# FFN second layer: the bias as a matmul of 33 rows, and the sum takes tn itself

## The reference, cut to what matters

```
tn  = _ln_t(t)                               # layer norm without gain
# each sample picks 2 of 8 experts, with weights top_w
h   = gelu(tn @ W1[e] + b1[e])               # 256 -> 512, for both experts
y   = h @ W2[e] + b2[e]                      # 512 -> 256
out = sum over the two experts of top_w * y
t   = t + _layer_norm(out + tn, gamma, beta)
```

## Time and profile before

| | us |
|---|---|
| median of 3 runs (1199.36 to 1202.1) | 1199.42 |
| the profiled execution | 1207.64 |
| its span | 1205.8 |
| TensorE busy, matmuls | 1060.5 |
| DVE busy | 701.9 |
| ACT busy | 514.0 |
| POOL busy, of which `tnb` 59.0 | 237.5 |

### The profile page before, as it was taken

How to read it: one execution, slowest core, us unless ns; L and a number is a source line. 1 busy time by engine, 2 the same in 40 slices (tenths; PEclk the granted TensorE clock), 3 DMA queues, 4 the chain that set the end, 5 groups by cost and what they waited for, 6 DMA issues and landing times. The chain is left out here.

```text
span 1205.8 us, 18621 instructions
## 1 busy us (share of the span) xinstructions
PE 1060.5 (88%) x6960; PEld 916.2 (76%) x6960; DVE 701.9 (58%) x1678; ACT 514.0 (43%) x963; POOL 237.5 (20%) x164
## 2 busy tenths in 40 slices
PE   3787999999999999928977765998999889989997
PEld 3776677667666666628876765998999889989997
DVE  3564444365355234235688745568677767767676
ACT  4564322333232201115455426655556464646542
POOL 1010100001000000040055542123233213323232
PEclk9788999999999999855688766999999999999999
DMA  9411112021102000033288734032032113201101
GB/s 249 130 40 40 40 40 75 5 86 48 40 3 75 18 1 17 1 107 95 65 247 248 210 91 132 25 108 53 27 90 88 36 28 110 74 26 53 27 28 40
DMA packets 99985, 87.91 MB, mean 73 GB/s; under 512 B 24793, under 2 KB 96762, under 8 KB 99804
## 3 DMA queue, kind: packets, MB, share of 16 engines
q1 hardware_dynamic: 89870, 76.79, 23.0%
q10 hardware_dynamic: 10032, 10.04, 2.5%
HBM read 56.62 MB, written 30.19 MB: 72 GB/s over the span
## 5 line engine op out<-in xcount | busy, mean ns | idle before, releaser
L706 PE MATMUL pM<-V,U 128*128 128x368 f16 (+3 forms) x2016 | 320.9, 316 | 0.0
L706 PEld LDWEIGHTS pM<-V,U 128*128 128x128 f16 x2016 | 197.4, 98 | 108.2 <-issue 1.6
L1517 DVE TENSOR_TENSOR gl<-gf,gh 128x384 fp32r<-128x384 f32 x192 | 162.9, 870 | 63.5 <-ACT gh L1395 63.5
L1395 ACT ACTIVATE gf<-pH,b1c 128x384 f32<-128x384 f32 x192 | 112.1, 584 | 173.0 <-PE pH L1630 84.5
L1645 PE MATMUL pY<-w2h,gh 128*128 128x256 f32 x576 | 168.8, 293 | 16.7 <-DVE z L1529 15.8
L1645 PE MATMUL pY<-w2l,gh 128*128 128x256 f32 x576 | 164.3, 285 | 0.0
L1645 PE MATMUL pY<-w2h,gl 128*128 128x256 f32 x576 | 164.0, 285 | 0.0
L510 DVE TENSOR_TENSOR V<-pV,V 128x384 f16<-128x384 f32 x96 | 53.1, 554 | 165.0 <-ACT V L408 165.0
L1630 PE MATMUL pH<-xh,w1h 128*128 128x384 f32 x384 | 132.5, 345 | 14.0 <-DVE w1l L1488 6.4
L408 ACT CAST V<-pV 128x384 f16<-128x384 f32 x96 | 45.8, 478 | 212.1 <-PE pV L677 212.1
L1630 PE MATMUL pH<-xl,w1h 128*128 128x384 f32 x384 | 131.7, 343 | 0.0
(11 more groups left out here) (177 smaller groups left out, 1526.7 us busy)
## 6 DMA issues: line engine op xcount, KB each, us to landing
xa<-in_xt SPq DMA_DIRECT2D x16, 576.0 KB, 4.9
xn_scratch<-xa SPq DMA_DIRECT2D x16, 576.0 KB, 6.1
tk<-t_scratch SPq DMA_DIRECT2D x24, 384.0 KB, 3.3
out<-o SPq DMA_DIRECT2D x24, 384.0 KB, 2.5
xn<-xn_scratch SPq DMA_DIRECT2D x16, 480.0 KB, 4.5
xr<-in_xt SPq DMA_DIRECT2D x16, 480.0 KB, 5.8
t_scratch<-ts ACTq DMA_DIRECT2D x16, 480.0 KB, 5.9
w1r<-in_ew SPq DMA_DIRECT2D x8, 512.0 KB, 4.1
```

The lines of the kernel that those rows point to most:

```text
L706: return nc.tensor.matmul(out[:, :, first:end], U[:, hi_u, k, piece, :], V[:, b % 2, hi_v, k, c, :, first + TILES * d:end + TILES * d], st ...
L1395: last = nc.scalar.activation(dst, pH[:, j % 4, 0:CN], ACT.Gelu, bias=b1c[:, j // FB, j % FB:j % FB + 1])
L1517: tt(gl[:, sl, j, :], gf[:, j % 2, :], gh[:, sl, j, :].bitcast(F32), ALU.subtract).then_inc(g_step, 1)
```

## The change

POOL no longer makes `tnb`, and the buffer goes. The weighted bias enters pY as the first product of each group: `onesr` (33 rows of ones, 128 columns) times `b2p` (33 rows, 256 columns), whose row 0 is the bias rounded to the matmul's type, whose row 32 is what the rounding left, and whose other rows are zero. DVE makes the two rows in `row_bias`, once per sample: ahead of `split_w2`, three operations one after another. `onesr` and the zeros of `b2p` are set once. `add(t)` adds pY and tnk; since tnk lives longer, it has 6 buffers. The waits follow: `sum_up` on `tn_made`, `normalise` on z's step Z_VE of six chunks before, SP on half the count of `bias_added`, TensorE on `row_step` at a sample's first chunk.

```diff
--- before.py
+++ after.py
@@ -1172,8 +1172,10 @@
 CHUNKS = SB // CN
 JB = TOPK * FB
 R_STEPS = 21
+BIAS_STEPS = 3
 TBUFS = CHUNKS
-NBUFS = 3
+NBUFS = CHUNKS
+BROW = 33
 AHEAD = 4
 
 Z_VE = 3 * CT + 1
@@ -1210,7 +1212,9 @@
         tk = sb("tk", [P, TBUFS, CT, C], F32)
         tnk = sb("tnk", [P, NBUFS, CT, C], F32)
         tb = sb("tb", [P, 2, CT, C], F32)
-        tnb = sb("tnb", [P, 2, CT, C], F32)
+        b2p = sb("b2p", [BROW, C], F32R)
+        b2h = sb("b2h", [BROW, C], F32R)
+        onesr = sb("onesr", [BROW, P], F32R)
         xh = sb("xh", [P, 2, CC, CN], F32R)
         xl = sb("xl", [P, 2, CC, CN], F32R)
         gf = sb("gf", [P, 2, CN], F32)
@@ -1242,6 +1246,8 @@
         w1_step = sem("w1_step")
         w2_step = sem("w2_step")
         bias_step = sem("bias_step")
+        row_set = sem("row_set")
+        row_step = sem("row_step")
         tk_loaded = [sem(f"tk_loaded{s}") for s in range(TBUFS)]
         tn_made = sem("tn_made")
         x_turned = sem("x_turned")
@@ -1264,7 +1270,7 @@
                 n, s = CHUNKS * b + m, m % TBUFS
                 if not is_first(b):
                     sp.wait_ge(tn_made, 2 * (n - TBUFS + 1))
-                    sp.wait_ge(bias_added, 2 * (n - TBUFS + 1))
+                    sp.wait_ge(bias_added, n - TBUFS + 1)
                 rows = ds(n * CN, CN)
                 sp.dma_start(tk[:, s], t_d[rows, :].rearrange("(t p) c -> p t c", p=P)).then_inc(tk_loaded[s], 16)
                 for w in range(2):
@@ -1324,14 +1330,9 @@
             def add_bias(b, m):
 
                 n, s = CHUNKS * b + m, m % 2
-                if m == 0:
-                    pool.wait_ge(bias_step, 3 * (b + 1))
-                pool.wait_ge(tn_made, 2 * (n + 1))
                 pool.wait_ge(tk_loaded[m % TBUFS], 48 * (CHUNKS // TBUFS * b + m // TBUFS + 1))
                 if not (is_first(b) and m < 2):
                     pool.wait_ge(z_step, (n - 1) * Z_ALL)
-                nc.gpsimd.tensor_tensor(tnb[:, s], tnk[:, m % NBUFS], b2c[:, 1:2, :].broadcast_to([P, CT, C]),
-                                        ALU.add).then_inc(bias_added, 1)
                 nc.gpsimd.tensor_tensor(tb[:, s], tk[:, m % TBUFS], bet[:, None, :].broadcast_to([P, CT, C]),
                                         ALU.add).then_inc(bias_added, 1)
 
@@ -1401,7 +1402,7 @@
                 act.wait_ge(tk_loaded[m % TBUFS], 48 * (CHUNKS // TBUFS * b + m // TBUFS + 1))
                 if not (is_first(b) and m < NBUFS):
                     act.wait_ge(x_turned, 2 * (n - NBUFS + 1))
-                    act.wait_ge(bias_added, 2 * (n - NBUFS + 1))
+                    act.wait_ge(z_step, (n - NBUFS) * Z_ALL + Z_VE)
                 for t in range(CT):
                     last = nc.scalar.activation(tnk[:, m % NBUFS, t, :], tk[:, m % TBUFS, t, :], ACT.Identity,
                                                 bias=xs[:, m % TBUFS, 1, t:t + 1], scale=xs[:, m % TBUFS, 0, t:t + 1])
@@ -1411,7 +1412,7 @@
             normalise(0, 1)
             take_x(0, 0)
             split_w1(0)
-            act.wait_ge(bias_step, 3)
+            act.wait_ge(bias_step, BIAS_STEPS)
             gelus(0, 0)
             take_x(0, 1)
             act.wait_ge(r_step, R_STEPS + 1)
@@ -1424,7 +1425,7 @@
                         split_w2(b)
                     if later(b, m, 1, CHUNKS):
                         if m == CHUNKS - 1:
-                            act.wait_ge(bias_step, 3 * (b + 2))
+                            act.wait_ge(bias_step, BIAS_STEPS * (b + 2))
                         gelus(*later(b, m, 1, CHUNKS))
                     if later(b, m, 3, CHUNKS):
                         normalise(*later(b, m, 3, CHUNKS))
@@ -1486,10 +1487,10 @@
                 for k in range(TOPK):
                     dve.wait_ge(w1hi_ready, TOPK * b + k + 1)
                     tt(w1l[:, k], w1r[:, k], w1h[:, k].bitcast(F32), ALU.subtract).then_inc(w1_step, 1)
-                s = Steps(dve, bias_step, b, 3)
+                s = Steps(dve, bias_step, b, BIAS_STEPS)
                 dve.wait_ge(b_loaded, 64 * (b + 1))
                 if not is_first(b):
-                    dve.wait_ge(bias_added, 2 * CHUNKS * b)
+                    dve.wait_ge(row_step, 3 * b)
                     dve.wait_ge(gelu_done, JB * CHUNKS * b)
                 s.did(nc.vector.tensor_copy(b1c[:, :, :], b1r[:, :, :]))
                 s.did(nc.vector.tensor_scalar(b2c[:, 0, :], b2r[:, 0, :], wbc[:, ds(TOPK * b, 1)], None,
@@ -1497,6 +1498,17 @@
                 s.settle()
                 s.did(stt(b2c[:, 1, :], b2r[:, 1, :], wbc[:, ds(TOPK * b + 1, 1)], b2c[:, 0, :],
                           ALU.mult, ALU.add))
+
+            def row_bias(b):
+                s = Steps(dve, row_step, b, 3)
+                dve.wait_ge(bias_step, BIAS_STEPS * (b + 1))
+                if not is_first(b):
+                    dve.wait_ge(y_ready, CT * CHUNKS * b)
+                s.did(nc.vector.tensor_copy(b2h[:, :], b2c[0:BROW, 1, :]))
+                s.settle()
+                s.did(nc.vector.tensor_copy(b2p[0:1, :], b2h[0:1, :].bitcast(F32)))
+                s.did(tt(b2p[BROW - 1:BROW, :], b2c[BROW - 1:BROW, 1, :], b2h[BROW - 1:BROW, :].bitcast(F32), ALU.subtract))
+                s.at(3)
 
             def split_w2(b):
                 for k in range(TOPK):
@@ -1522,11 +1534,11 @@
                 n, sl = CHUNKS * b + m, m % 2
                 s = Steps(dve, z_step, n, Z_ALL)
                 s.settle()
-                dve.wait_ge(bias_added, 2 * (n + 1))
+                dve.wait_ge(tn_made, 2 * (n + 1))
 
                 def add(t):
                     dve.wait_ge(y_ready, CT * n + t + 1)
-                    s.did(tt(z[:, t, :], pY[:, (CT * m + t) % 2, 0:C], tnb[:, sl, t, :], ALU.add))
+                    s.did(tt(z[:, t, :], pY[:, (CT * m + t) % 2, 0:C], tnk[:, m % NBUFS, t, :], ALU.add))
 
                 def stats(t):
                     s.did(nc.vector.bn_stats(st[:, t, :], z[:, t, :]))
@@ -1561,16 +1573,24 @@
                 s.at(Z_ALL)
 
             half = JB // 2
+            dve.wait_ge(c_set, 2)
+            nc.vector.tensor_copy(onesr[:, :], ones[0:BROW, :]).then_inc(row_set, 1)
+            nc.vector.memset(b2c[:, 0, :], 0.0).then_inc(row_set, 1)
+            dve.wait_ge(row_set, 2)
+            nc.vector.tensor_copy(b2p[:, :], b2c[0:BROW, 0, :]).then_inc(row_set, 1)
+            dve.wait_ge(row_set, 3)
             take_x(0, 0)
             split_w1(0)
             split_hidden(0, 0, range(JB))
             take_x(0, 1)
+            row_bias(0)
             split_w2(0)
 
             def body(b):
                 for m in range(CHUNKS):
 
                     if m == 0 and not is_first(b):
+                        row_bias(b)
                         split_w2(b)
                     if later(b, m, 1, CHUNKS):
                         split_hidden(*later(b, m, 1, CHUNKS), range(half))
@@ -1636,15 +1656,17 @@
                 pe.wait_ge(g_step, JB * (n + 1))
                 if m == 0:
                     pe.wait_ge(w2_step, 2 * (b + 1))
+                    pe.wait_ge(row_step, 3 * (b + 1))
                 for t in range(CT):
                     if not (is_first(b) and m == 0 and t < 2):
 
                         pe.wait_ge(z_step, (n - 1) * Z_ALL + 2 * t + 2 if t < 2 else n * Z_ALL + 1)
                     terms = [(j, g, w) for j in range(JB) for g, w in ((gh, w2h), (gh, w2l), (gl, w2h))]
+                    nc.tensor.matmul(pY[:, (CT * m + t) % 2, 0:C], onesr[:, :], b2p[:, :], start=True, stop=False)
                     for i, (j, g, w) in enumerate(terms):
                         last = nc.tensor.matmul(pY[:, (CT * m + t) % 2, 0:C], g[:, s, j, t * P:(t + 1) * P],
                                                 w[:, j // FB, j % FB, :],
-                                                start=(i == 0), stop=(i == len(terms) - 1))
+                                                start=False, stop=(i == len(terms) - 1))
                     last.then_inc(y_ready, 1)
 
             turn_x(0, 0)
```

## The result

The changed kernel takes 1224.5 us (median of 6 runs, 1219.1 to 1227.2), the kernel before in the same sessions 1201.4 (6 runs). The ratio is 1.0185, 95% interval 1.0149 to 1.0220: 22 us slower. The profiled execution is 1224.02 us long, its span 1222.2.

The account below looks back on a forecast made before the run. In the FFN TensorE bounds, waiting for z's sums on DVE. 35.5 - 1.2 + 3.6 - 5.5 - 7.9 - 2.1 = +22.4 us on the median of 1199.4 gives 1221.8; range 1202 to 1237, first rival included.

Parts of the forecast that it names:

- The dear product: 72 added 33-row products empty TensorE on both sides: 0.525 us each, 0.43 at t = 0, +35.5 us in all.
- The end-to-load distance of 0.07 us: Behind a 49-row product the next weight load begins 0.07 us before that product ends; taken to hold for 33 rows.
- the rival without emptying: On TensorE, 33-row products go through like 96 rows, 8.5 us in all: sum +3.1, 1202.5 us; chance 0.12.
- Waits given back: TensorE's waits for z at t = 2: 14 short ones vanish (-5.5 us), seven long ones shrink (-7.9); emptyings hidden in six (-1.2).
- The clock given back: Behind the three switch waits, shrunk to about 2.3 us, TensorE's granted clock falls less: half of 3 x 1.4, -2.1 us.
- row_bias: Its three DVE operations stand on the path at the start of samples 2 to 4: 3 x 1.2 = +3.6 us.
- the three set-up operations: At the start, on DVE: they fall into its idle time ahead of `xl` while the first weights load, costing nothing.
- the removal of `tnb`: On POOL, read in a quiet chunk: saves 1.6 us of DVE time, but at most 0.3 us on the path.
- the likeliest case: Emptying as summed: 1221.8 us, own range given as 1207 to 1237; chance 0.80.
- Relief of DVE: Rival: waits at t = 2 all hang on POOL holding DVE up, so all come back: 1185 us; `xh` against it; chance 0.04.
- the 1.5 named as a sign: On DVE in the new profile, `gl` of over 1.5 us should be one per chunk, not two.

Follow-up runs that it names:

- e1: The changed kernel with onesr and b2p of 128 rows instead of 33, added b2p rows zero: chunks 437.6 us, ratio 1.0004 to the kernel before.
- e2: The changed kernel with onesr and b2p of 65 rows instead of 33: chunks 439.0 us, one execution, no ratio.
- e5: The changed kernel with POOL's wait for the bias and `tnb` back in the first two chunks: start 28.2 us, chunks 461.0 us, one execution.
- e6: The changed kernel with POOL's `tnb` back in all chunks, into a buffer nothing reads: start 27.9 us, chunks 461.1 us, one execution.

## Why the prediction was right

**The dear product: right, in mechanism and size.** Of the 22.4 us forecast the largest term was 0.525 us for each product at t = 1 and 2, and the timeline bears it out: from one bias product to the next (1160.49 to 1163.84) it is 3.35 us, and 24 ordinary steps are 2.84 (22 of them, 1161.03 to 1163.63, are 2.60), which leaves 0.51. At t = 0 it is 0.50 and not 0.43: from the first of the six transposes to the second ordinary product 1.28 us instead of 0.78. Together 48 x 0.51 + 24 x 0.50 = 36.5 us instead of 35.5. The end-to-load distance of 0.07 us, read off one transpose of 49 rows, was the decisive row, and the steps of 0.21 and 0.31 us exclude the rival without emptying; e1 and e2 show that the row count makes them.

**Waits given back: right.** Six are left, as forecast; in gaps between starts and with the restart behind each, 22.3 us fell to 7.8. That is 14.5 for the 13.4 and 1.2 forecast.

**The clock given back: right in direction, too small.** The slow products fell from 6.7 to 1.3 us, so 5.4 came back and not 2.1. Before there were 5.1 us of them behind the three switch waits, where the forecast had 4.2, and 1.6 more behind a wait in layer 1 at 992 us, which it left out. After, the clock fell behind one of the three switch waits of 2.0 us. In e5, with waits as long, it fell behind all three, and 4.1 us of slow products are left there: that would have been 2.6 given back, near the forecast. The matmuls behind the three waits in the changed kernel (busy, count, granted clock, DMA share, GB/s):

```profile
842.10:846.90 4.80, 4.74 (x25) 0.64 0.01 3
962.40:965.70 3.30, 3.26 (x26) 1.00 0.00 0
1085.60:1089.00 3.40, 3.31 (x26) 1.00 0.00 0
```

and in e5; so how much comes back differs from one execution to the next:

```profile
837.90:841.80 3.90, 3.87 (x19) 0.61 0.00 0
958.20:962.10 3.90, 3.88 (x18) 0.56 0.00 0
1083.10:1087.00 3.90, 3.90 (x22) 0.69 0.00 0
```

**row_bias: right in place and, at two samples of three, in size.** Its three operations take 1.0 us, and 1.2 (sample 2) and 1.1 (sample 4) from the first one's start to `w2l`'s. TensorE's waits in layer 1, read as gaps between starts, rose there from nothing to 1.1 and 1.0 us. At sample 3, where the loop goes round for the second time, they rose by 2.4, from 3.2 to 5.5: 4.5 in all instead of 3.6. It was not seen that DVE stands idle there twice with nothing to wait for in the profile (2.98 and 1.82 us, before once for 3.30) and TensorE twice (1.81 and 0.86, before not at all). Why, no run shows; that the engines fetch their instructions there would fit.

**Missed: longer steps in layer 1.** The steps of products of 384 columns are 0.002 us longer than before, 2.0 us over all chunks, told of at the end.

**Missed: the start.** That the three set-up operations there cost nothing was true, and nothing else at the start entered the sum. The step that failed there is the removal of `tnb`, read in a quiet chunk alone: `add_bias` of the first chunk loses its wait for the bias too, `tb` moves some 14 us forward (from 4.2 us behind the first product of layer 1 to 9.8 ahead of it), and DVE's first `gl` come free. That is worth 3.9 us. e5 shows it, and so does the table: the four kernels with these sums at the old place start in 27.2 to 28.2 us, all others in 23.2 to 24.6.

**How much of it is luck.** The terms as measured are 36.5 for the products, 14.5 and 5.4 given back, 4.5 and 2.0 lost in layer 1: 23.1 where the chunks took 22.6. So the forecast's 22.4 is the chunks' number, right to 0.2 us by some luck, since 3.3 us too little for the clock stand against 3.9 us too little for products, row_bias and longer steps. The start takes 3.9 off, 18.8 in all by the two traces; the ratio's 22 us, with an interval from 18 to 26, takes in both. Of the medians, 1221.8 was forecast from 1199.4, and 1224.5 stands against 1201.4. The path and the two large terms were right, and with them the direction.

**Small slips in the working.** By its own terms the range of the likeliest case is 1207.8 to 1238.0, not 1207 to 1237, and a held `gl` ends 0.4 us behind the POOL operation (16.90 and 16.48), not 0.5. Neither changes the forecast.

**Relief of DVE: right that it hangs on `xh`.** Shown by the wait of 1.22 us in front of `xl` and by e6. The `gl` that is still held takes 1.4 us, a little less than the 1.5 named as a sign.

## What to carry to other kernels

Before a product of few rows is put between full ones, look in the trace for the weight load behind any such product: if it starts only as that product ends, pad the rows with zeros up to 65 or more, or don't put it there. Before work is taken off an engine because its neighbour is late, ask for which of the neighbour's operations the bottleneck waits, and whether that one can simply go first: here this gave about 2% where the exchange cost about 2%. A removed wait acts at the program's start as well as in its steady part, and both are to be read.

## What was not expected of the hardware

Products of 384 columns that follow one another without a gap step 0.1734 us (47 steps in 8.15) in some chunks and 0.1766 (8.30) in others. In the changed kernel every chunk ahead of which TensorE had not waited has the longer one; behind a wait, and in the kernel before, both occur (0.1743 on average before, 0.1762 after). It makes some 2 us of the loss, and no run here tells why. Otherwise the border: a product of 65 rows costs what one of 128 does, and one of 33 rows over four times as much (0.12 and 0.51 us).
